# One more adder chunk on GpSimd, a new table of places in the attention loop, and weight halves awaited one by one

## The chip, the cores and the metric

The kernel runs on one core of a Trainium2 chip. The metric is device microseconds of one execution; before the change three runs gave a median of 1325.45 us (1325.14 to 1329.71). The engines are PE (TensorE), DVE (VectorE), ACT (ScalarE) and POOL (GpSimd); SP and ACT issue the DMAs.

## The reference

Two sequences of 1024 tokens with 1024 features go through one layer norm, then through an attention branch and a linear branch that are added to the input.

```
xn  = layernorm(x)
q, k, v = split(clip(xn @ Wqkv.T, -8, 8));  q, k = layernorm(q)*w+b, layernorm(k)*w+b
scores = q @ k.T / sqrt(32) + slope[h] * (pos_k - pos_q), causal     # 32 heads of 32
out = x + (softmax(scores) @ v) @ Wout.T + xn @ (alpha * sign(Wffn)).T + bias
```

## The kernel before, in words

**Blocks.** PE forms five products of 16 token tiles (128 tokens each) with 1024 x 1024 weights: F (the sign weights), Q, K, V, and after the attention the output product. `product` (L1079 on) goes over eight steps k; a step reads the two weight halves (columns 0 to 511 and 512 to 1023) of row block k, each kept as a high and a low fp16 part. ACT writes the high part (`split_hi`), DVE the low part (`split_lo`, L864, semaphore `w_lo`). Half number t of the next block is split while tile t of this block is worked on, after DVE has taken tile t out of PSUM (`clipped`, L940). Ahead of Q, of K and of V, PE waits until all 16 low halves are there. A product of tile t needs the PSUM banks of tile t-2 to be emptied.

**Attention.** 16 groups (n) of four heads follow. A group has 12 chunks c: chunks 0 to 3 are key tiles 0 to 3 of the first query half, chunks 4 to 11 are key tiles 0 to 7 of the second. A chunk is 512 query columns wide, or 384, 256 and 128 for the last tiles of a half (chunks 1, 2, 3 and 9, 10, 11). A place (c, j) is chunk c with head j. All engines go through fixed orders of work; semaphores alone tie them together. On PE, at each place:

- `scores` (L1206, with a mask product L1209 on the diagonal) writes one of three PSUM banks; it waits until the exponential (ACT, `exps`, L793) three places earlier has ended.
- 42 items of group n+1 are spread over the places of group n by `NATS`, the number of items in each chunk. 40 items are products (`maxima`, L1151) from which DVE takes row maxima (L988, L992); items 2 and 15 turn a row of them (L1158). They use three banks of their own: item i waits until DVE is done with item i-3. After item 41 DVE takes the minimum of two sets of 16 values (`both_halves`, L998), and item 2 of the next group's places waits for that minimum.
- `with_v` (L1229) multiplies the exponentials of a chunk with V into bank O, late, at the places that `PV_AFTER` gives (-2 and -1 are chunks 10 and 11 of the group before). The first of a group waits until ACT has copied bank O out for the last half (`os_copy` of half 1, L801). `DIRECT` chunks are also summed over keys by fp32 products with ones (L1235), into bank S.

**Sums on POOL.** For the chunks in `ADDED` POOL adds the exponentials into one tile (`add_in`, L641), and one product with ones (L1239, behind chunk 11's `with_v`) sums that tile. For the first half POOL adds chunks 1 and 2 to chunk 0 (`add_first`, L651), and `sums_first` (L1248) sums the result. The order on POOL in a group n > 0 is: `o_norm(n-1, 0)` (L620), add_first 1, add_first 2, `o_low(n-1, 0)` (L630), add 6, add 7 (chunk numbers), `o_norm(n-1, 1)`, add 9, `o_low(n-1, 1)`. `add_first` waits for the `with_v` of chunk 0. ACT's `os_copy(n, 0)` writes the buffer that `o_low(n-1, 0)` reads, and waits for it. Buffers of exponentials are reused: `HELD` names the chunk whose products and adds must be over before a chunk is written. Sums leave by `sums0_copy`, a DMA, `recips` on DVE, two more DMAs, and come back to `o_norm`.

Of the kernel before, what the change touches and what calls it, by code (L numbers as in the profile page):

```python
# [14 lines left out]
NT = TOK // P  # L15
KT = DM // P
QT = SEQ // P
# [12 lines left out]
def ready(n, ring=RING):  # L30

    return n + 1 + ring


def slot_free(n):

    return n + 1


def stored(j):  # L40


    return 16 * j + 16
# [23 lines left out]
def build_program(nc, x, wqkv_t, wout_t, wffn_t, ffn_bias, q_w, q_b, k_w, k_b,  # L67
# [9 lines left out]
    with ctx:  # L77
# [110 lines left out]
        def sem(name):  # L188
            return ctx.enter_context(nc.semaphore(name))
# [29 lines left out]
        w_lo = sem("w_lo")  # L219
# [49 lines left out]
        F, Q, K, V, WO = range(5)  # L269
# [20 lines left out]
        def span(c):  # L290
# [1 line left out]
            at = max(0, P * t - HALF * qb)  # L292
            return qb, t, at, HALF - at

        NATS = [3, 4, 3, 4, 3, 4, 4, 4, 5, 3, 2, 3]
        assert sum(NATS) == ITEMS


        PV_AFTER = {(0, 2): [-2], (2, 1): [-1], (3, 0): [0], (4, 2): [1], (5, 2): [2], (5, 3): [3],
                    (7, 1): [4], (8, 1): [5], (9, 0): [6], (9, 3): [7], (10, 2): [8], (11, 1): [9]}  # L300

        def due(c, j):

            return sum(NATS[:c]) + NATS[c] * (j + 1) // GH

        ADDED = (1, 2, 3, 5)
        DIRECT = [t not in (ADDED if qb else (0, 1, 2)) for qb, t in CHUNKS]
        ADDS = len(ADDED) - 1  # L310
        ADDS0 = 2
        FIRST_ADDS = {3: [1, 2]}

# [5 lines left out]
        def slot(c):  # L321
            i, col = SLOT[c]
            return p32[i][:, :, col:col + span(c)[3]]

        def adds_for(k):

            n, c = k // NC, k % NC
            return ADDS * n + max(1, ADDED.index(CHUNKS[c][1])) if CHUNKS[c] in [(1, t) for t in ADDED] else 0

# [20 lines left out]
        def need(eng, s, v):  # L350
            if v > 0:
                eng.wait_ge(s, v)
# [201 lines left out]
        def _(pool):  # L554
# [60 lines left out]
            def o_norm(n, qb):  # L615

                m = blk_no(n, qb)
                pool.wait_ge(r_ld[m % 2], 16 * (m // 2 + 1))
                o = os_sb[m % 2][:, 0, :]
                nc.gpsimd.tensor_tensor(o, o, rb[m % 2], ALU.mult).then_inc(on_done, 1)  # L620

            def o_low(n, qb):

                m = blk_no(n, qb)
                pool.wait_ge(oh_done, m + 1)
                if (n, qb) == (0, 0):
                    for s in range(2):
                        pool.wait_ge(v_st[s], stored(NT // 2))
                part = [ot[n][:, s, qb * HALF:(qb + 1) * HALF] for s in range(2)]
                nc.gpsimd.tensor_tensor(part[1], os_sb[m % 2][:, 0, :], part[0], ALU.subtract).then_inc(ol_done, 1)  # L630

            def add_in(n, c):

                qb, t, at, w = span(c)
                k = n * NC + c
                pool.wait_ge(exp_done, GH * (k + 1))
                if t == ADDED[1]:
                    need(pool, pv_done, n * NC)
                need(pool, add_done, adds_for(k) - 1)
                former = slot(c - 1) if t == ADDED[1] else acc[:, :, at:HALF]  # L640
                nc.gpsimd.tensor_tensor(acc[:, :, at:HALF], former, slot(c), ALU.add).then_inc(add_done, 1)  # L641

            def add_first(n, c):

                at = span(c)[2]
                k = n * NC + c
                pool.wait_ge(exp_done, GH * (k + 1))
                pool.wait_ge(pv_done, n * NC + 1)
                need(pool, add0_done, adds0_for(k) - 1)
                total = slot(0)[:, :, at:HALF]  # L650
                nc.gpsimd.tensor_tensor(total, total, slot(c), ALU.add).then_inc(add0_done, 1)  # L651

            for n in range(GROUPS):
                for c in range(NC):
                    if CHUNKS[c] in [(1, t) for t in ADDED[1:]]:
                        add_in(n, c)
                    for first in FIRST_ADDS.get(c, []):
                        add_first(n, first)
                    if n > 0:
                        if c == 0:  # L660
                            o_norm(n - 1, 0)
                        if c == 5:
                            o_low(n - 1, 0)
                        if c == 7:
                            o_norm(n - 1, 1)
                        if c == 11:
                            o_low(n - 1, 1)
            def resid(t):
                p = t % 2
# [20 lines left out]
        def _(act):  # L690
# [83 lines left out]
            for t in range(NT):  # L774
                p, j = t % 2, t // 2
# [46 lines left out]
            for n in range(GROUPS):  # L822
                for c in range(NC):
                    for j in range(GH):
                        exps(n, c, j)
                        if n > 0:
                            if (c, j) == (2, 1):
                                o_high(n - 1, 0)
                            if (c, j) == (2, 1):
                                os_copy(n - 1, 1)  # L830
                            if (c, j) == (11, 0):
                                o_high(n - 1, 1)
                            if j == 3 and 0 < c <= LOADS and n + 2 < GROUPS:
                                load_part(act, n + 2, c - 1)
                            if (c, j) == (LOADS + 1, 3) and n < GROUPS - 1:
                                if n == 1:
                                    for s in range(2):
                                        act.wait_ge(v_st[s], stored(NT // 2))
                                load_vg(act, n + 1)
                        if (c, j) == (6, 2):  # L840
                            os_copy(n, 0)
                        if (c, j) == (6, 2):
                            sums0_copy(n)
            os_copy(GROUPS - 1, 1)
            o_high(GROUPS - 1, 0)
# [4 lines left out]
        def _(dve):  # L850
# [168 lines left out]
            for t in range(NT):  # L1019
                p, j = t % 2, t // 2  # L1020
# [16 lines left out]
            for n in range(GROUPS):  # L1037
                for pos in range(ITEMS):
                    if n < GROUPS - 1:
                        nat_item(n + 1, pos)  # L1040
                    elif pos == 0:
                        row_out(n, use(GROUPS, 0), row_b, rowb_ld)
                    if pos == 18 and n > 0:
                        recips(n - 1, 1)
                    if pos == 33:
                        recips(n, 0)

            def c_out_step(t, p):
# [13 lines left out]
        def _(pe):  # L1062
# [41 lines left out]
            def block_product(blk, t, p, between=None, tile=None):  # L1104
                pe.wait_ge(mm_out, slot_free(t + NT * blk))
                product([ps[:, 2 * p + c, :] for c in range(2)],
                        lambda k, a: xnt[:, bass.ds(t if tile is None else tile, 1), k, a, :].rearrange("p o c -> p (o c)"),
                        wsl[blk % 2], TWO if blk == F else THREE, between).then_inc(mm_done, 1)
# [23 lines left out]
            pe.wait_ge(const_ld, 16 * 3)  # L1132
            pe.wait_ge(alpha_set, 1)

            for blk in (Q, K):
                pe.wait_ge(w_lo, ready(NT * blk - 1))

                def step(t, p, j, first=False):
                    block_product(blk, t, p, tile=p * QT + j)

                tile_loop(pe, step)

# [34 lines left out]
                    maxima(s, pos)  # L1177


            pe.wait_ge(w_lo, ready(NT * V - 1))  # L1180
            for t in range(NT):
                if t < V_FIRST:
                    block_product(V, t, t % 2)
                    continue
                if t == V_FIRST:
                    pe.wait_ge(fill_ld, 16 * 2 * STACKS)

                def between(k):
                    for pos in range(due_in_v(t, k - 1), due_in_v(t, k)):
                        nat_item(0, pos)  # L1190

                block_product(V, t, t % 2, between)
# [61 lines left out]
            for n in range(GROUPS):  # L1254
                pe.wait_ge(rowa_ld, ROW_PARTS * (n + 1))
                for c in range(NC):
                    if c == QB_END[0] + 1:
                        pe.wait_ge(rowb_ld, ROW_PARTS * (n + 1))
                    for j in range(GH):
                        scores(n, c, j)  # L1260
                        if n < GROUPS - 1:
                            for pos in range(due(c, j - 1), due(c, j)):
                                nat_item(n + 1, pos)
                        elif (c, j) == (0, 0):
                            row_b_turn(n, use(GROUPS, 0))
                        for late in PV_AFTER.get((c, j), []):
                            if n > 0 or late >= 0:
                                with_v(n * NC + late)
                        if (c, j) == (6, 2):
                            sums_first(n)  # L1270


# [77 lines left out]
```

## Time and profile before

| | before |
|---|---|
| median of 3 runs | 1325.45 us |
| profiled execution, its own time | 1327.45 us |
| its span | 1325.4 us |
| PE, DVE, POOL, ACT busy | 97%, 61%, 43%, 38% |
| mean granted TensorE clock | 0.995 |
| Q, K, V stages | about 147 to 671 us |
| attention | 672.7 to 1152.7 us |
| output product | to the end |

Busy is the share of the span in which an engine had an instruction running. PE's instructions are pipelined and their ends are modelled, so on PE the distance from one start to the next says more than a duration. "idle before" with a releaser names what ended an engine's wait.

### The profile page before, as it was taken

The numbers are of one execution on the slowest core, as the hardware profiler recorded it, in microseconds if no ns is written. First come the engines' busy times: TensorE is split into PE (matmuls) and PEld (weight loads), VectorE is DVE, ScalarE is ACT, GpSimd is POOL, SyncE is SP. The second block draws the span as 40 slices with busy tenths as digits, with TensorE's granted clock in tenths as the row PEclk, the third lists the DMA queues.
The fourth block names the chain that finished last, engine by engine and source line by source line (L and its number), as shares of the span: only waits on it lengthen the run. The fifth ranks groups of instructions, "written<-read, shape, count | busy, mean of one in ns | idle before, by whom it ended". The sixth has DMA issues, their size and how long they took to land.

```text
span 1325.4 us, 35664 instructions
## 1 busy us (share of the span) xinstructions
PE 1289.3 (97%) x14628; PEld 640.9 (48%) x14628; DVE 808.0 (61%) x1811; ACT 510.1 (38%) x1018; POOL 574.8 (43%) x360
## 2 busy tenths in 40 slices
PE   5999999998999989999999999999999999999998
PEld 3455444443444434444356655555555555444443
DVE  4656378876877772123688888888888888011111
ACT  6444011111111110000057777777777777600000
POOL 5562000000000000000037777777777777797674
PEclk9999999999999989999999999999999999999999
DMA  6545122222222225922114333444443331344443
GB/s 238 197 159 192 62 71 73 74 77 70 68 77 78 77 80 133 218 72 72 65 50 85 89 87 85 92 99 91 104 100 91 87 90 38 114 140 155 143 144 126
DMA packets 167718, 137.97 MB, mean 104 GB/s; under 512 B 116273, under 2 KB 132785, under 8 KB 167346
## 3 DMA queue, kind: packets, MB, share of 16 engines
q1 hardware_dynamic: 68020, 99.55, 25.2%
q10 hardware_dynamic: 99566, 36.50, 12.3%
q8 instruction: 102, 1.67, 0.6%
q14 instruction: 30, 0.25, 0.1%
HBM read 93.42 MB, written 42.21 MB: 102 GB/s over the span
## 4 chain that ended last, share of the span: by engine, by line
PE 94%; DVE 2%; DMA 1%; issue 1%; POOL 1%; ACT 1%; SPq 0%; DVEq 0%; ACTq 0%; POOLq 0%
PE ps L1085 59%; PE ps L1151 9%; PE ps L1206 9%; PE ps L1229 9%; PE ps L1235 3%; PE ps L1209 2%; PE ps L1074 1%; PE ps L1248 1%; PE ps L1239 1%; DMA arena<-arena 1%; DVE ps L988 1%; DMA arena<-in_x 0%; POOL arena L651 0%; SPq L470 0%; DVE arena L940 0%
## 5 line engine op out<-in xcount | busy, mean ns | idle before, releaser
L1085 PE MATMUL ps<-arena 128*128 128x512 f16 x3584 | 786.9, 381 | 9.3 <-DVE arena L864 9.0
L1085 PEld LDWEIGHTS ps<-arena 128*128 128x128 f16 (+1 forms) x3584 | 348.6, 98 | 434.7 <-issue 15.4
L793 ACT ACTIVATE arena<-ps 128x512 f32<-128x512 f32 (+3 forms) x768 | 333.1, 499 | 122.1 <-PE ps L1209 69.1
L988 DVE CUSTOM_DVE_ANT_0 ps<-ps,arena 128x128 f32<-128x128 f32 (+3 forms) x512 | 238.4, 517 | 37.0 <-PE ps L1151 36.8
L1206 PE MATMUL ps<-arena 128*32 128x512 f16 (+3 forms) x3072 | 256.8, 327 | 3.6 <-DVE arena L940 1.4
L1151 PE MATMUL ps<-arena 127*32 127x512 f16 (+3 forms) x3072 | 237.8, 328 | 0.6 <-DVE arena L988 0.4
L641 POOL TENSOR_TENSOR arena<-arena 128x2048 f32<-128x2048 f32 (+1 forms) x48 | 202.8, 4226 | 37.5 <-ACT arena L793 35.0
L651 POOL TENSOR_TENSOR arena<-arena 128x1536 f32<-128x1536 f32 (+1 forms) x32 | 93.8, 2930 | 262.5 <-PE ps L1229 190.0
L992 DVE TENSOR_REDUCE arena<-ps 128x1 f16<-128x512 f32 x256 | 166.7, 687 | 47.8 <-PE ps L1151 47.7
L564 POOL TENSOR_TENSOR small<-small 128x1 f32<-128x1 f32 x48 | 19.5, 407 | 386.6 <-DVE small L876 384.9
L1229 PE MATMUL ps<-arena 128*32 128x512 f32 (+3 forms) x1536 | 160.6, 486 | 0.5 <-issue 0.3
L940 DVE TENSOR_SCALAR arena<-ps 128x1024 f32<-128x1024 f32 x48 | 58.8, 1224 | 144.0 <-PE ps L1085 133.9
L1206 PEld LDWEIGHTS ps<-arena 128*32 128x32 f16 x3072 | 93.0, 96 | 76.5 <-issue 28.3
L751 ACT ACTIVATE arena<-arena 128x1024 f16<-128x1024 f32 x32 | 33.8, 1056 | 247.2 <-DVE arena L976 247.2
L1209 PE MATMUL ps<-arena 128*32 128x128 bf16 x2048 | 120.7, 218 | 0.0
L701 ACT ACTIVATE arena<-arena 128x512 f32 (+1 forms) x64 | 40.0, 627 | 205.3 <-DMA arena<-in_wout_t 151.5
L1052 DVE SCALAR_TENSOR_TENSOR arena<-ps,arena 128x1024 f32<-128x1024 f32 x16 | 19.6, 1224 | 152.6 <-PE ps L1085 130.0
L1151 PEld LDWEIGHTS ps<-arena 127*32 127x32 f16 x3072 | 83.9, 96 | 51.8 <-issue 14.6
L1209 PEld LDWEIGHTS ps<-arena 128*32 128x32 bf16 x2048 | 63.1, 97 | 47.1 <-issue 27.6
L988 DVE DVE_READ_ACCUMULATOR2_ANT arena<- 128x1 f16 x512 | 72.9, 142 | 0.0
L871 DVE BATCH_NORM_STATS2 small<-arena 128x6 f32<-128x512 f32 x96 | 61.6, 683 | 6.3 <-DMA arena<-in_x 5.2
L969 DVE SCALAR_TENSOR_TENSOR arena<-arena,small 128x1024 f32<-128x1024 f32 x32 | 41.1, 1284 | 33.3 <-POOL small L610 33.3
(55 smaller groups left out, 848.1 us busy)
## 6 DMA issues: line engine op xcount, KB each, us to landing
arena<-in_x SPq DMA_DIRECT2D x32, 512.0 KB, 5.3
arena<-in_wqkv_t SPq DMA_DIRECT2D x48, 256.0 KB, 6.1
base_scr<-arena SPq DMA_DIRECT2D x16, 512.0 KB, 2.9
v_scr<-arena SPq DMA_DIRECT2D x16, 512.0 KB, 3.0
arena<-r_scr SPq DMA_DIRECT2D x32, 256.0 KB
arena<-base_scr SPq DMA_DIRECT2D x16, 512.0 KB, 4.0
out_dram<-arena SPq DMA_DIRECT2D x16, 512.0 KB, 6.2
arena<-v_scr ACTq DMA_DIRECT2D x14, 512.0 KB, 4.2
```

Of the source, the lines that this page charges most:

```text
L641: nc.gpsimd.tensor_tensor(acc[:, :, at:HALF], former, slot(c), ALU.add).then_inc(add_done, 1)
L651: nc.gpsimd.tensor_tensor(total, total, slot(c), ALU.add).then_inc(add0_done, 1)
L793: nc.scalar.activation(slot(c)[:, j, :], ps[:, TRB[x % RB], 0:w], ACT.Exp, scale=SCALE).then_inc(exp_done, 1)
L871: ins = nc.vector.bn_stats(bst[p][:, 6 * c:6 * c + 6], xc[p][:, c * HALF:(c + 1) * HALF])
L940: nc.vector.tensor_scalar(dst[p], banks(2 * p, 2), lim, -lim, ALU.min, ALU.max)\
L988: ins = nc.vector.tensor_tensor_reduce(tile, tile, mnat[:, HALF - width:HALF], scale=-1.0, scalar=3e38, op0=ALU.add, op1=ALU.min, accum_ou ...
L992: ins = nc.vector.tensor_reduce(negm[s % 2][:, at:at + 1], tile, AX, ALU.max, negate=True)
L1085: ins = nc.tensor.matmul(dst[c], lhs(k, a), wparts[:, k, b, c * HALF:(c + 1) * HALF], start=(k == 0 and (a, b) == order[0]), stop=(k == KT ...
L1151: ins = nc.tensor.matmul(by_tile(dst), q[0:P - 1, r // DH, i, j], tiles_of(k[0:P - 1], j, key, width), start=True, stop=True)
L1206: ins = nc.tensor.matmul(by_tile(dst), k[:, r // DH, t, j], tiles_of(q, j, q0, w), start=True, stop=not diagonal)
L1209: ins = nc.tensor.matmul(dst[:, 0:P], idb[:, r:r + DH], mtr, start=False, stop=True)
L1229: ins = nc.tensor.matmul(dst(O_BANK, j, at), v[:, t, j, :], p[:, j, :], start=first, stop=last)
```

## The change

`ADDED` gets chunk (1, 6), which is chunk 10. So POOL also adds chunk 10 into the tile (256 columns for each of four heads), between add 9 and `o_low(n-1, 1)`; PE no longer forms chunk 10's four fp32 products with ones; PE's product L1239 waits for one add more, and ACT's chunk 2 of the next group, which reuses the buffer, waits for the add. `FIRST_ADDS`, and the places of `o_norm` and `o_low`, move in POOL's text, though except for the new add the order of POOL's instructions stays as it was. `NATS`, `PV_AFTER` and the places of ACT's and DVE's copies change. The wait for all 16 weight halves becomes a wait for each step's two halves in the first tile of Q, K and V.

```diff
-        NATS = [3, 4, 3, 4, 3, 4, 4, 4, 5, 3, 2, 3]
+        NATS = [2, 4, 2, 4, 4, 5, 5, 2, 3, 4, 5, 2]
-        PV_AFTER = {(0, 2): [-2], (2, 1): [-1], (3, 0): [0], (4, 2): [1], (5, 2): [2], (5, 3): [3],
-                    (7, 1): [4], (8, 1): [5], (9, 0): [6], (9, 3): [7], (10, 2): [8], (11, 1): [9]}
+        PV_AFTER = {(0, 2): [-2], (2, 2): [-1], (3, 0): [0], (3, 3): [1], (4, 3): [2], (5, 2): [3],
+                    (7, 2): [4], (8, 0): [5], (9, 0): [6], (9, 3): [7], (10, 2): [8], (11, 2): [9]}
-        ADDED = (1, 2, 3, 5)
+        ADDED = (1, 2, 3, 5, 6)
-        FIRST_ADDS = {3: [1, 2]}
+        FIRST_ADDS = {3: [1], 5: [2]}
@@ POOL: o_norm(n-1, 0), o_norm(n-1, 1), o_low(n-1, 1) in the loop over c
-   c == 0, c == 7, c == 11
+   c == 2, c == 8, c == 10
@@ ACT
-   o_high(n-1, 0) at (2, 1); os_copy(n-1, 1) at (2, 1); o_high(n-1, 1) at (11, 0)
+   o_high(n-1, 0) at (3, 2); os_copy(n-1, 1) at (2, 2); o_high(n-1, 1) at (10, 3)
-   os_copy(n, 0) at (6, 2); sums0_copy(n) at (6, 2)
+   os_copy(n, 0) at (6, 0); sums0_copy(n) at (6, 3)
@@ DVE
-                    if pos == 18 and n > 0: recips(n - 1, 1)      ... pos == 33: recips(n, 0)
+                    if pos == 19 and n > 0: recips(n - 1, 1)      ... pos == 34: recips(n, 0)
@@ PE
+            def weights(blk, k):
+                pe.wait_ge(w_lo, ready(NT * (blk - 1) + 2 * k + 1))
             for blk in (Q, K):
-                pe.wait_ge(w_lo, ready(NT * blk - 1))
+                weights(blk, 0)
                 def step(t, p, j, first=False):
-                    block_product(blk, t, p, tile=p * QT + j)
+                    block_product(blk, t, p, (lambda k: weights(blk, k + 1)) if first else None, p * QT + j)
-            pe.wait_ge(w_lo, ready(NT * V - 1))
+            weights(V, 0)                                          # and the same between in V's tile 0
-                        if (c, j) == (6, 2): sums_first(n)
+                        if (c, j) == (6, 1): sums_first(n)
```

## Rows read from the trace of the kernel before

**Rows 1.** Stretch of one attention group: length, busy time of each engine, clock, DMA.
```profile
1019.39:1049.45 30.06, 30.06 (x679) 16.82 (x674) 25.63 (x86) 23.57 (x56) 23.28 (x10) 1.00 0.42 93
```

**Rows 2.** Waits of PE: total us, times, longest.
```profile
PE ps L1085 <- DVE arena L864: 9.0, 2, 4.5
```

**Rows 3.** DVE in order of time, block ends: start, us, work [idle before].
```profile
302.12 1.22 DVE L940 TENSOR_SCALAR arena<-ps 128x1024 f32<-128x1024 f32 x1 [0.66 <-PE ps L1085]
...
312.48 1.22 DVE L940 TENSOR_SCALAR arena<-ps 128x1024 f32<-128x1024 f32 x1 [0.94 <-PE ps L1085]
...
328.96 1.23 DVE L940 TENSOR_SCALAR arena<-ps 128x1024 f32<-128x1024 f32 x1 [7.14 <-PE ps L1085]
...
484.36 1.23 DVE L940 TENSOR_SCALAR arena<-ps 128x1024 f32<-128x1024 f32 x1 [0.94 <-PE ps L1085]
...
502.03 1.22 DVE L940 TENSOR_SCALAR arena<-ps 128x1024 f32<-128x1024 f32 x1 [8.32 <-PE ps L1085]
...
524.23 1.22 DVE L940 TENSOR_SCALAR arena<-ps 128x1024 f32<-128x1024 f32 x1 [10.05 <-DMA v_scr<-arena]
```

**Rows 4.** Stretch behind the first wait: length, PE busy, granted clock, DMA, GB/s.
```profile
317.00:319.00 2.00, 2.00 (x5) 0.50 0.52 135
```

**Rows 5.** PE in order of time, a late group (product with V of chunk 4; then from place (0, 0)).
```profile
1021.28 1.04 PE L1229 MATMUL ps<-arena 128*32 128x512 f32 x8
...
1034.54 0.40 PE L1206 MATMUL ps<-arena 128*32 128x512 f16 x4
...
1036.13 0.61 PE L1235 MATMUL ps<-arena 128*32 128x256 f32 x8
1036.56 0.40 PE L1206 MATMUL ps<-arena 128*32 128x512 f16 x4
...
1036.84 0.22 PE L1158 MATMUL ps<-arena 128*16 128x128 f16 x1
...
1039.23 0.40 PE L1229 MATMUL ps<-arena 128*32 128x128 f32 x8
...
1041.54 1.04 PE L1229 MATMUL ps<-arena 128*32 128x512 f32 x8
```

**Rows 6.** POOL in order of time, the same group.
```profile
1021.93 9.34 POOL L641 TENSOR_TENSOR arena<-arena 128x2048 f32<-128x2048 f32 x2 [2.09 <-ACT arena L793]
...
1032.44 3.52 POOL L641 TENSOR_TENSOR arena<-arena 128x1536 f32<-128x1536 f32 x1
1035.90 1.17 POOL L630 TENSOR_TENSOR arena<-arena 128x512 f16<-128x512 f32 x1
...
1046.40 2.38 POOL L651 TENSOR_TENSOR arena<-arena 128x1024 f32<-128x1024 f32 x1 [0.17 <-POOL arena L651]
1048.74 1.16 POOL L630 TENSOR_TENSOR arena<-arena 128x512 f16<-128x512 f32 x1
```

**Rows 7.** DVE's minimum of the same group.
```profile
1035.76 0.23 DVE L998 TENSOR_TENSOR arena<-arena 128x16 f16<-128x16 f16 x1
```

**Rows 8.** An early group: DVE's minimum.
```profile
734.16 1.11 DVE L998 TENSOR_TENSOR arena<-arena 128x16 f16<-128x16 f16 x1
```

**Rows 9.** The early group: POOL.
```profile
734.05 1.19 POOL L630 TENSOR_TENSOR arena<-arena 128x512 f16<-128x512 f32 x1
```

**Rows 10.** All sixteen of DVE's minima: ns least/median/most, first and last start.
```profile
L998 DVE TENSOR_TENSOR arena<-arena x16: 167/222/1171, 671.0 to 1125.9; 128x16 f16<-128x16 f16 x16
```

**Rows 11.** The early group: PE, item 3.
```profile
735.97 0.40 PE L1151 MATMUL ps<-arena 127*32 127x512 f16 x4 [0.21 <-DVE arena L988]
```

**Rows 12.** The last group: ACT's copy of bank O behind chunk 11's product.
```profile
1131.67 0.60 ACT L801 ACTIVATE arena<-ps 128x512 f32<-128x512 f32 x1 [0.33 <-PE ps L1239]
```

**Rows 13.** The last group: PE, chunk 11's product with V, then chunk 0's.
```profile
1130.12 0.40 PE L1229 MATMUL ps<-arena 128*32 128x128 f32 x8
...
1132.37 1.07 PE L1229 MATMUL ps<-arena 128*32 128x512 f32 x8 [0.32 <-issue]
```

**Rows 14.** ACT in order of time, a late group: three exponentials.
```profile
1021.21 1.63 ACT L793 ACTIVATE arena<-ps 128x512 f32<-128x512 f32 x3
```

More of the change, by code:

```diff
@@ L659, in _ @@
                     if n > 0:
-                        if c == 0:
+                        if c == 2:
                             o_norm(n - 1, 0)
@@ L663, in _ @@
                             o_low(n - 1, 0)
-                        if c == 7:
+                        if c == 8:
                             o_norm(n - 1, 1)
-                        if c == 11:
+                        if c == 10:
                             o_low(n - 1, 1)
@@ L826, in _ @@
                         if n > 0:
-                            if (c, j) == (2, 1):
+                            if (c, j) == (3, 2):
                                 o_high(n - 1, 0)
-                            if (c, j) == (2, 1):
+                            if (c, j) == (2, 2):
                                 os_copy(n - 1, 1)
-                            if (c, j) == (11, 0):
+                            if (c, j) == (10, 3):
                                 o_high(n - 1, 1)
@@ L839, in _ @@
                                 load_vg(act, n + 1)
-                        if (c, j) == (6, 2):
+                        if (c, j) == (6, 0):
                             os_copy(n, 0)
-                        if (c, j) == (6, 2):
+                        if (c, j) == (6, 3):
                             sums0_copy(n)
@@ L1042, in _ @@
                         row_out(n, use(GROUPS, 0), row_b, rowb_ld)
-                    if pos == 18 and n > 0:
+                    if pos == 19 and n > 0:
                         recips(n - 1, 1)
-                    if pos == 33:
+                    if pos == 34:
                         recips(n, 0)
@@ L1177, in nat_item @@
                     maxima(s, pos)
-            pe.wait_ge(w_lo, ready(NT * V - 1))
+            weights(V, 0)
             for t in range(NT):
                 if t < V_FIRST:
-                    block_product(V, t, t % 2)
+                    block_product(V, t, t % 2, (lambda k: weights(V, k + 1)) if t == 0 else None)
                     continue
@@ L1268, in _ @@
                                 with_v(n * NC + late)
-                        if (c, j) == (6, 2):
+                        if (c, j) == (6, 1):
                             sums_first(n)
```

## The prediction

> **What bounds the kernel now.** I read the busy shares first, then one attention group as a stretch, then PE's waits, then each engine in order of time. PE is busy for the whole of a group and no other engine is: DVE 25.6, ACT 23.6, POOL 23.3 of 30.06 us [rows 1]. PE's only long waits outside the start are two of 4.5 us for DVE's weight halves [rows 2], at the ends of Q and K. So the time is PE's work plus what makes PE wait, and the question is what the shorter order makes late.
>
> **Weight halves, a gain.** While a block runs, DVE takes a tile out each 10.36 us (302.12 to 312.48). From Q's last tile to K's first it is 16.48 us, from K's last to V's first 17.67 us [rows 3]. The excess is 6.12 and 7.31 us, more than the 4.5 us of waiting, because PE works on at the lower of its two clocks behind the wait: 0.50 granted, and 5 products in 2 us [rows 4]. PE had stood idle before that. Only the last low half is late, since half t is split behind tile t. With step waits PE comes to it at 7/8 of a tile, 9.1 us behind the block's end, and it is ready 4.5 us behind it: no wait, no idle, no lower clock. Q's first tile gains nothing, as no wait stands there [rows 2]. What is late next? DVE takes V's tile 2 out only when a store has landed, at 524.23 [rows 3]; PE needs that bank for tile 4, which starts at 525.8 if V follows K at once (four tiles behind 484.36). Even if the store did not move this holds by some 0.3 us, and the stores' chain hangs on V's tile 0 and moves too. Price if that cover failed: 1 us. The step waits themselves I put at 0: tiles with a wait each follow at 10.36 us (bounds 0 and 24 x 0.1 us, an estimate from the 0.10 us between the copy's end at 1132.27 and PE's start behind it [rows 12, 13]). Sum: **-13.4 us** (bounds -13.4 and -11.0).
>
> **Chunk 10's sums leave PE.** Four products of 256 columns, 1036.13 to 1036.56: 0.43 us in each group [rows 5], 16 groups, -6.9 us, if nothing takes its place. POOL's new add has the shape of 1046.40: 2.38 us [rows 6], and 0.17 us behind the add before it. 23.3 + 2.4 of 30 us would fit by the sum; its place decides.
>
> **Where the new add lies.** I count in a steady group from E, the end of the exponential at (6, 3). Add 6 starts 0.08 us behind E; from its start to the end of add 9 it is 14.03 us (1021.93 to 1035.96) [rows 6]. So add 9 ends at E + 14.1, add 10 runs from E + 14.3 to E + 16.7. On PE, chunk 4's product with V moves from (7, 1) to (7, 2), behind a score that needs the exponential of (6, 3): it starts no earlier than E + 0.27: that score's 0.22 us and 0.05 from release to start, half of the 0.10 that rows 12 and 13 show behind a copy (at 0.10 the new add only comes earlier). From it to the next group's first score, call that S, it is 13.26 us (1021.28 to 1034.54) [rows 5], less the 0.22 us score that now lies ahead: 13.04. So S = E + 13.3, add 9 ends at S + 0.8, and **add 10 runs from S + 0.95 to S + 3.33**. Before, add 9 ended at S + 1.42 and a short `o_low` of 1.17 us followed.
>
> **Who meets it.** DVE's minimum (L998) is ready at S + 1.22 (1035.76) [rows 7]; item 41 keeps its place against S, so 1.2 again. Its row ends at 1035.99, 0.03 us behind add 9's end. In the early group it started 0.11 us after `o_low` and took 1.11 us, to 735.27, again 0.03 us behind POOL's end at 735.24 [rows 8, 9]. The 16 minima take 0.17 to 1.17 us for the same 16 columns [rows 10]. I take it that this instruction, which reads two SBUF operands, waits for the POOL instruction in flight. Then it ends at S + 3.33 instead of S + 1.45.
>
> The Trainium skill's page "SBUF — State Buffer", section "Who interferes with whom", says that a DVE instruction with two SBUF inputs contends with a GpSimd instruction that reads SBUF, and that whichever issues first keeps the shared pair for its whole length. By that rule the blocked sum below holds (about 1338 us); by the reading that the long minima are chance, the free sum does (about 1317 us). The rows' 0.03 us ends bear the rule out.
>
> **What PE does then.** PE comes to item 2's turn at S + 2.30 - 0.43 = S + 1.9 (1036.84 is 2.30 behind 1034.54) [rows 5] and must wait for the minimum: 3.4. Item 3 started 0.70 us after the minimum's end in the early group (735.97) [rows 8, 11], so S + 4.03. To chunk 11's product it is 1.7 us of scores and items by widths (0.42 ns a column, from the 0.43 us for 4 x 256) and 0.2 us for ACT's pace: S + 5.9. Chunk 0's product follows at least 2.25 us later, for bank O's copy must be over: 1130.12, copy at 1131.67, product at 1132.37 [rows 12, 13]. (Before it was 2.31 us, with more scores between [rows 5]; now scores alone would give 1.96.) So chunk 0's product is at S + 8.15. From its start to the end of `o_low(n-1, 0)` it is 8.36 us (1041.54 to 1049.90) [rows 5, 6]. `os_copy(n, 0)`, moved from behind the exponential of (6, 2) to behind (6, 0), must wait for that: +0.08. A copy takes 0.60 us and three exponentials 1.63 [rows 12, 14], of which I let 0.15 overlap: the next E is 10.5 us behind chunk 0's product, S + 18.65. The group: 18.65 + 13.3 = **31.95 us, 1.9 more than 30.05**.
>
> If the minimum were free, ACT's pace would put chunk 11's product at 4.69 (1039.23) - 0.43 + 0.17 = S + 4.43, chunk 0's at 6.68, E at 17.2 and the group at **30.5 us**: the two waits on ACT and `o_low` take back more than the 0.43 us. That is the nearer bound of the cost of this step; the far one is 29.62 us, if no wait comes at all.
>
> **Sum.** Groups 2 to 14: 13 x 1.9 = 24.7, less 1 us, since two early groups pay part of it already [rows 8]: 23.7. Group 1, where POOL has no `o_norm` of half 1 and add 10 lies 1.3 us earlier: +0.5. Group 0: 0. Group 15 waits for the minimum at its first place, 1.9 us later than now, then copy and `o_low` as above, and PE saves 0.43 in the tail: together +1.5 (0 to 3). Attention +25.7, weights -13.4: **+12.3 us**. The profiled execution reports 1327.45 us around a span of 1325.4; the median of runs, 1325.45, equals the span, so I put the change on the median: 1337.8 us, given as 1338. The output product is PE's own work; POOL's last add delays its residual sums by 2.4 us, and the first tile taken out still precedes PE's need of its banks: 0.
>
> **Rivals.**
> - *The minimum is free.* For it: add 10 precedes the minimum by only 0.25 us; if the minimum arrives in the 0.17 us between the adds it slips through. Against: PE cannot start chunk 4's product before E + 0.27, so add 9 can't end later than S + 0.8. 13 x 0.45 less the share of the early groups that goes, + 0.5 for groups 1 and 15: +5 - 13.4 = -8.4, 1317 us. Chance 0.17.
> - *Nothing waits at all.* -13.4 - 6.9 = 1305 us. For it: PE shows no idle in steady groups. Against: bank O's copy already leaves 0.06 us (2.31 against 2.25). Chance 0.08.
> - *Only the weight part's gain goes*, V's store or the lower clock keeping half of it, with the blocked groups: 1345 us. Against: rows 3 as above. Chance 0.05.
> - *Blocked*, the forecast: 0.70, with its own range 1331 to 1343 (a group 31.4 to 32.3 us). It is the case on the slower side: from the point where add 10 starts ahead of the minimum, each group pays the rest of 2.38 us.
>
> **How the numbers follow.** The range reaches from the free case to the top of the blocked one: 1316 to 1343 us. Half a per cent, 6.6 us, is about what a measurement of this kernel tells from no change. Faster than 1318.8: the second rival and some two thirds of the first, 0.20. Within: the rest of the first and the blocked case's lower edge, 0.15. Slower than 1332.1: 0.65.
>
> **What would show it.** Right: DVE's tiles 10.4 us apart over both block ends, no lower clock there; L998 2 us long in groups 2 to 14, ending with a POOL add of 1024 columns; PE's L1158 about 3.4 us behind the group's first score; groups of about 32 us. Wrong: L998 at 0.2 us (then 30.5 or less for a group), `os_copy(n, 0)` starting without a wait, or an idle PE in V.

## The result, and the profile after

The changed kernel takes **1338.4 us** (median of four runs, 1337.9 to 1338.6), the kernel before beside it on the same chip 1327.1. The ratio is **1.008 (95%: 1.006 to 1.011)**: slower by 0.8%. The forecast was 1338 us, from an expected +12.3 us on 1325.45; between the two medians here it is +11.3 us, between the profiled spans 1336.9 - 1325.4 = +11.5 us. All readings below are of the profiled execution.

The busy shares, one engine after the other, for the whole span of the changed kernel: PE is at 97%, and nobody else has come near it.
```profile
PE 1291.8 (97%) x14500; PEld 617.6 (46%) x14500; DVE 828.6 (62%) x1811; ACT 509.5 (38%) x1018; POOL 610.4 (46%) x376
```

One group of attention in the columns of [rows 1], from one group's first score nearly to the next one's. PE is no longer busy throughout: 1.4 us of idle are new. POOL is 2.15 us busier, by the new add, and DVE 1.6 us, though it has no new work.
```profile
1005.15:1037.00 31.85, 30.42 (x670) 15.82 (x666) 27.23 (x86) 23.62 (x54) 25.43 (x11) 1.00 0.38 88
```

PE's waits (total us, times, longest), to be read against [rows 2]: the wait for L864 is gone, and one for the minimum, L998, has come.
```profile
PE ps L1162 <- DVE arena L998: 14.4, 12, 2.8
PE ps L1155 <- DVE arena L988: 2.6, 12, 0.2
```

**Where time was gained.** DVE's tiles taken out, where [rows 3] had the gaps: the last of K stands at 477.86 and the first of V at 488.32, 10.46 us apart where it was 17.67. Q's and K's tiles pass through at 10.36. The tile that waits for V's store (the last row) has moved forward by 11.7 us, from 524.23 to 512.54, nearly as far as the chain, and PE waits nowhere in V.
```profile
301.74 1.23 DVE L940 TENSOR_SCALAR arena<-ps 128x1024 f32<-128x1024 f32 x1 [0.65 <-PE ps L1085]
312.10 1.23 DVE L940 TENSOR_SCALAR arena<-ps 128x1024 f32<-128x1024 f32 x1 [0.94 <-PE ps L1085]
...
477.86 1.23 DVE L940 TENSOR_SCALAR arena<-ps 128x1024 f32<-128x1024 f32 x1 [0.94 <-PE ps L1085]
488.32 1.23 DVE L940 TENSOR_SCALAR arena<-ps 128x1024 f32<-128x1024 f32 x1 [1.12 <-PE ps L1085]
...
512.54 1.23 DVE L940 TENSOR_SCALAR arena<-ps 128x1024 f32<-128x1024 f32 x1 [12.07 <-DMA v_scr<-arena]
```

The stretch of [rows 4], read in the same way: 11 products in 2 us where there were 5, at a granted clock of 1.00 (2.4 GHz) where it was 0.50.
```profile
317.00:319.00 2.00, 2.00 (x11) 1.00 0.60 145
```

DVE takes V's last tile out 13.7 us earlier, at 657.70 against 671.41, and PE's first score of attention is as far ahead: 658.97 against 672.69.

**Where it was lost.** PE in the same order as [rows 5], in the group that begins at S = 1005.15. The turn of item 2 (L1162) waits 1.05 us for the minimum; the products with V (L1233) of chunks 11, 0 and 4 stand at 1011.00, 1013.24 and 1024.07.
```profile
1005.15 0.40 PE L1210 MATMUL ps<-arena 128*32 128x512 f16 x4
...
1008.46 0.22 PE L1162 MATMUL ps<-arena 128*16 128x128 f16 x1 [1.05 <-DVE arena L998]
...
1009.12 0.40 PE L1155 MATMUL ps<-arena 127*32 127x512 f16 x4 [0.21 <-DVE arena L988]
...
1011.00 0.40 PE L1233 MATMUL ps<-arena 128*32 128x128 f32 x8
...
1013.24 1.07 PE L1233 MATMUL ps<-arena 128*32 128x512 f32 x8 [0.15 <-issue]
...
1024.07 1.03 PE L1233 MATMUL ps<-arena 128*32 128x512 f32 x8
...
1037.10 0.40 PE L1210 MATMUL ps<-arena 128*32 128x512 f16 x4
```

POOL in the same stretch, against [rows 6]. One row holds adds 9 and 10; it ends at 1008.38.
```profile
1002.40 5.98 POOL L641 TENSOR_TENSOR arena<-arena 128x1536 f32<-128x1536 f32 x2
1008.34 1.16 POOL L630 TENSOR_TENSOR arena<-arena 128x512 f16<-128x512 f32 x1
```

DVE's minimum of this group, against [rows 7]: ready at S + 1.13, 2.13 us long for the same 16 columns, over at 1008.41, 0.03 us behind POOL.
```profile
1006.28 2.13 DVE L998 TENSOR_TENSOR arena<-arena 128x16 f16<-128x16 f16 x1
```

All sixteen minima, against [rows 10]: the median went from 222 to 2129 ns.
```profile
L998 DVE TENSOR_TENSOR arena<-arena x16: 168/2129/2144, 657.3 to 1134.1; 128x16 f16<-128x16 f16 x16
```

From group to group, by the start of POOL's row that holds `add_first` 2, the fifteen lengths sum to 453.8 us before and 477.8 after. Before they are 31.1, 30.7, 30.7, then 30.0 to 30.1, at the end 30.7. After they are 31.9 to 32.1, with two of 30.53 and 30.54 (groups 2 and 10), and 33.3 at the end. In the two short ones the minimum slipped through, as here (DVE, then POOL's row of adds 9 and 10, then add 10 by itself): it started between the two adds, 0.02 us ahead of add 10.
```profile
721.51 0.17 DVE L998 TENSOR_TENSOR arena<-arena 128x16 f16<-128x16 f16 x1
```
```profile
717.91 6.02 POOL L641 TENSOR_TENSOR arena<-arena 128x1536 f32<-128x1536 f32 x2
```
```profile
721.53 2.40 POOL L641 TENSOR_TENSOR arena<-arena 128x1024 f32<-128x1024 f32 x1
```
The minimum was no earlier there (S + 1.13, as elsewhere); add 10 was later, at S + 1.15 instead of S + 0.88. The delay begins between adds 6 and 7 of the groups just before (1 and 9): they stand 0.44 us apart there and 0.14 us in all others (one row). Group 9, then group 10:
```profile
966.39 4.58 POOL L641 TENSOR_TENSOR arena<-arena 128x2048 f32<-128x2048 f32 x1 [0.43 <-ACT arena L793]
```
```profile
991.92 9.30 POOL L641 TENSOR_TENSOR arena<-arena 128x2048 f32<-128x2048 f32 x2 [2.23 <-ACT arena L793]
```
The exponential that the row names was over by 964.92, so it is not what add 7 waited for. The same pause of 0.3 us stands in groups 1 and 9, and in no other, of all ten kernels in which POOL adds chunk 10 as one instruction, and in no group of the other four (before, e1, e5, e6). What makes it is not known.

The last group, beside [rows 13]: the turn waits 2.83 us there, and a product with ones (L1252) 0.47 for POOL's last add.
```profile
1136.20 0.22 PE L1162 MATMUL ps<-arena 128*16 128x128 f16 x1 [2.83 <-DVE arena L998]
...
1149.63 1.07 PE L1252 MATMUL ps<-arena 128*32 128x384 f32 x16 [0.47 <-POOL arena L651]
```

### The profile page after: what moved, and what is told of

Same layout as the page of the kernel before. It is cut to its first block, busy times and chain, and to the rows that moved or that the text cites. A ratio compares the mean times of both kernels' runs of the same rounds, so it can differ in the third digit from the quotient of the medians.

```text
span 1336.9 us, 35440 instructions
## 1 busy us (share of the span) xinstructions
PE 1291.8 (97%) x14500; PEld 617.6 (46%) x14500; DVE 828.6 (62%) x1811; ACT 509.5 (38%) x1018; POOL 610.4 (46%) x376
## 4 chain that ended last, share of the span: by engine, by line
PE 91%; DVE 5%; issue 2%; ACT 1%; DMA 1%; POOL 0%; SPq 0%; DVEq 0%; ACTq 0%; POOLq 0%
PE ps L1085 58%; PE ps L1155 9%; PE ps L1233 8%; PE ps L1210 8%; PE ps L1239 3%; DVE ps L988 2%; PE ps L1213 1%; PE ps L1074 1%; DVE arena L998 1%; PE ps L1252 1%; PE ps L1243 1%; ACT arena L793 1%; DVE arena L992 1%; DVE arena L988 0%; DMA arena<-arena 0%
## 5 line engine op out<-in xcount | busy, mean ns | idle before, releaser
L641 POOL TENSOR_TENSOR arena<-arena 128x2048 f32<-128x2048 f32 (+1 forms) x64 | 239.9, 3749 | 43.3 <-ACT arena L793 38.8
L1155 PE MATMUL ps<-arena 127*32 127x512 f16 (+3 forms) x3072 | 228.9, 328 | 3.6 <-DVE arena L988 2.6
L992 DVE TENSOR_REDUCE arena<-ps 128x1 f16<-128x512 f32 x256 | 162.8, 688 | 36.3 <-PE ps L1155 35.0
L1233 PE MATMUL ps<-arena 128*32 128x512 f32 (+3 forms) x1536 | 159.4, 487 | 2.9 <-issue 2.2
L1210 PEld LDWEIGHTS ps<-arena 128*32 128x32 f16 x3072 | 88.0, 96 | 78.5 <-ACT arena L793 48.0
L1155 PEld LDWEIGHTS ps<-arena 127*32 127x32 f16 x3072 | 78.4, 95 | 78.5 <-DVE arena L988 28.1
L1213 PEld LDWEIGHTS ps<-arena 128*32 128x32 bf16 x2048 | 59.5, 97 | 46.9 <-issue 29.9
```

The costliest lines, as they stand in the source:

```text
L992: ins = nc.vector.tensor_reduce(negm[s % 2][:, at:at + 1], tile, AX, ALU.max, negate=True)
L1155: ins = nc.tensor.matmul(by_tile(dst), q[0:P - 1, r // DH, i, j], tiles_of(k[0:P - 1], j, key, width), start=True, stop=True)
L1210: ins = nc.tensor.matmul(by_tile(dst), k[:, r // DH, t, j], tiles_of(q, j, q0, w), start=True, stop=not diagonal)
L1213: ins = nc.tensor.matmul(dst[:, 0:P], idb[:, r:r + DH], mtr, start=False, stop=True)
L1233: ins = nc.tensor.matmul(dst(O_BANK, j, at), v[:, t, j, :], p[:, j, :], start=first, stop=last)
```

## The experiments

Each ran beside the kernel before. The ratio is to that kernel, with its 95% interval. "Step waits" are the change's weight waits alone; all kernels below but e2 have them. The table puts one late group of each kernel (about 1000 to 1060 us) into four stretches, from starts on PE: the group's first score, the product with V of chunk 11 (of the group before), of chunk 0, of chunk 4, the next first score.

| kernel | places | add 10 | minimum | to chunk 11 | to chunk 0 | to chunk 4 | to the score | group |
|---|---|---|---|---|---|---|---|---|
| before | old | no | two operands | 4.69 | 2.31 | 9.79 | 13.26 | 30.05 |
| after | new | yes | two | 5.85 | 2.24 | 10.83 | 13.03 | 31.95 |
| e3 | new | yes | one | 4.44 | 2.24 | 10.83 | 13.03 | 30.54 |
| e4 | old | yes | two | 4.26 | 3.30 | 9.82 | 13.27 | 30.65 |
| e8 | old, `o_high` later | yes | one | 4.28 | 2.29 | 9.80 | 13.26 | 29.63 |
| e9 | new, late ones undone | yes | one | 4.45 | 2.24 | 10.57 | 13.25 | 30.51 |
| e10 | new, early ones undone | yes | one | 4.27 | 2.25 | 10.82 | 13.02 | 30.36 |
| e11 | new, items old | yes | one | 4.72 | 2.24 | 11.01 | 12.96 | 30.93 |
| e12 | as e9, items old | yes | one | 4.72 | 2.25 | 9.98 | 13.41 | 30.36 |

**e1: the weight waits alone.** The kernel before with
```
- pe.wait_ge(w_lo, ready(NT * blk - 1))
+ weights(blk, 0)      # and weights(blk, k + 1) before step k + 1 of the first tile
```

> The kernel before with the step waits for weight halves alone. All theories: DVE takes tiles out 10.36 us apart over both block ends (before 16.48 and 17.67), no lower clock there; 13.4 us less than before, ratio 0.990. If the table or the add interacts with it, the difference of this run and the next from the whole change would not add up.

1314.65 us, ratio 0.990 (0.987 to 0.993). From Q's tile at 303.75 to V's first at 490.33 it is 186.58 us, 13.3 less than before, as in the changed kernel. Groups are 30.05 us, as before, but for one more of 30.6 (group 10), in which the minimum took 1.16 us. The clock behind Q's end, in the columns of [rows 4]:
```profile
317.00:319.00 2.00, 2.00 (x11) 1.00 0.25 86
```
The weight part is a gain of its own, and the only part of the change that is one as it stands.

**e2: the table alone.** The changed kernel with the old wait for the last half: the edit of e1 reversed.

> The changed kernel with the old wait for all weight halves: the add on POOL and the new places alone. If the parts are independent: 25 us more than before, ratio 1.019, groups of 31.8 us, L998 at 2.13 us. If the gain at the block ends were not what the changed kernel shows, this run would stay near it (ratio 1.008).

1353.49 us, ratio 1.020 (1.018 to 1.022). Waits of PE:
```profile
PE ps L1158 <- DVE arena L998: 14.5, 12, 2.8
PE ps L1085 <- DVE arena L864: 9.0, 2, 4.5
```
The two parts do not touch: 0.990 x 1.020 = 1.010 beside the whole change's 1.008 (1.006 to 1.011). DVE's tiles over the two block ends are 17.71 us (314.86 to 332.57) and 16.61 us (487.97 to 504.58) apart here, where the kernel before had 16.48 and 17.67 [rows 3]: the same two waits, but the dearer one now comes first.

**e3: the changed kernel, the minimum with one operand.** The two rows of 16 that the minimum compares lie side by side, so one reduction over a strided view gives the same result, into columns of its own:
```
- nc.vector.tensor_tensor(negm[n % 2][:, 16:32], negm[n % 2][:, 16:32], negm[n % 2][:, 32:48], ALU.min)
+ nc.vector.tensor_reduce(negb[n % 2], negm[n % 2][:, 16:48].rearrange("p (a b) -> p b a", a=2), AX, ALU.min)
```

> The changed kernel, but DVE forms the minimum as a reduction over one strided operand into its own 16 columns, in place of an operation with two SBUF operands. Port theory (the two-operand instruction waits for the POOL instruction in flight): the minimum takes 0.2 to 0.3 us, PE no longer waits for it, groups fall from 31.8 to 30.5 us, and the whole is 8 us less than before (ratio 0.994). Rival (the moved places cost the time, and the minimum's length is a symptom): no change, ratio 1.008. Rival (DVE or SBUF is slow for any instruction beside POOL's add): the reduction takes 2 us as well, ratio 1.008.

1321.01 us, ratio 0.996 (0.994 to 0.997), groups 30.53 us. All sixteen, then the one of a late group, and POOL beside it:
```profile
L999 DVE TENSOR_REDUCE arena<-arena x16: 185/187/189, 657.6 to 1118.5; 128x16 f16<-128x32 f16 x16
```
```profile
1026.61 0.19 DVE L999 TENSOR_REDUCE arena<-arena 128x16 f16<-128x32 f16 x1
```
```profile
1022.73 6.02 POOL L642 TENSOR_TENSOR arena<-arena 128x1536 f32<-128x1536 f32 x2
```
The reduction starts and ends in the middle of POOL's second add (1026.4 to 1028.75) and takes 0.19 us. So the 2.13 us were neither the work of a minimum nor a semaphore's delay, and DVE is not slow beside POOL's add in general. The edit changes three things at once, though: the number of SBUF operands, the operation, and the place of the result (no longer over an operand). The runs alone do not say which of them counts. This one instruction is worth 17.4 us (1338.4 to 1321.0), more than the change costs.

The Trainium skill's page "SBUF — State Buffer", section "Who interferes with whom", says this of both forms: `tensor_tensor` with both inputs in SBUF contends with GpSimd's reads, `tensor_reduce` on trn2 never does. The runs agree: 2129 ns in the median against 187 ns, under the same add. That the two operands are what counts rests on this page.

**e4: the new add in the old places.** The kernel before with the step waits and `ADDED = (1, 2, 3, 5, 6)`, nothing moved.

> The kernel before with step waits and with chunk 10 added on POOL, all places as in before, the two-operand minimum kept. Port theory: add 9 still ends 1.4 us behind a group's first score, the minimum is ready at 1.2 and goes between the two adds, so it takes 0.2 to 0.3 us; but the add delays o_norm(n-1, 0) by 2.5 us to 6.4 us, o_high stands before the copy of bank O at (2, 1), and chunk 0's product comes at 7.7 in place of 6.6: groups of 30.7 us, 4 us less than before in all (ratio 0.997). Rival (POOL's larger load costs it wherever the places are): L998 of 2 us, groups near 31.8, ratio 1.008. Rival (nothing waits with the old places): groups of 29.6, ratio 0.985.

1319.4 us, ratio 0.994 (0.992 to 0.996). The minimum is ready just before add 9 ends and goes first (DVE; then POOL, where the first add of the row ends at about 1029.92):
```profile
1029.72 0.25 DVE L998 TENSOR_TENSOR arena<-arena 128x16 f16<-128x16 f16 x1
```
```profile
1026.44 6.01 POOL L641 TENSOR_TENSOR arena<-arena 128x1536 f32<-128x1536 f32 x2
1032.42 1.17 POOL L630 TENSOR_TENSOR arena<-arena 128x512 f16<-128x512 f32 x1
1033.54 1.28 POOL L620 TENSOR_TENSOR arena<-arena 128x512 f32<-128x512 f32 x1
```
What is late instead is `o_high(n-1, 0)` at (2, 1): ACT stands 1.51 us there for POOL, and chunk 0's product behind it waits (ACT, then PE).
```profile
1034.86 0.63 ACT L817 ACTIVATE arena<-arena 128x512 f16<-128x512 f32 x1 [1.51 <-POOL arena L620]
```
```profile
1036.07 1.07 PE L1233 MATMUL ps<-arena 128*32 128x512 f32 x8 [0.82 <-issue]
```
So the add does not pay in the old table as it stands, for a reason that has nothing to do with the minimum: in the table above the second stretch is 3.30 us instead of 2.31.

**e5: the changed kernel, add 10 in two.** In `add_in`, the last of `ADDED` as two instructions of two heads each:
```
+ for js in (slice(0, 2), slice(2, 4)):
+     ins = nc.gpsimd.tensor_tensor(acc[:, js, at:HALF], acc[:, js, at:HALF], slot(c)[:, js], ALU.add)
+ ins.then_inc(add_done, 1)
...
```

> The changed kernel with add 10 given as two POOL instructions, one for heads 0 and 1 and one for heads 2 and 3; the two-operand minimum kept. Port theory, held for one instruction: the minimum waits for the first of the two only, so it takes about 1.0 us in place of 2.13, PE's turn of item 2 comes at 2.3 us behind the group's first score in place of 3.3, groups of 30.8 us, ratio to before 0.998. Rival (the minimum waits until POOL's queue is empty or until add 10's semaphore is given, for some ordering reason): 2.1 us or more, ratio 1.008 or above.

1326.21 us, ratio 1.000 (0.999 to 1.001); groups 30.87 us. DVE, then POOL:
```profile
1032.55 1.06 DVE L1003 TENSOR_TENSOR arena<-arena 128x16 f16<-128x16 f16 x1
```
```profile
1032.30 2.52 POOL L642 TENSOR_TENSOR arena<-arena 128x512 f32<-128x512 f32 x2
```
The minimum waits for the half that is in flight and no longer for the whole: the length of POOL's instruction sets its time.

**e6: the new places without the add.** The changed kernel with `ADDED = (1, 2, 3, 5)`.

> The changed kernel without the add: all new places and the step waits, but PE forms chunk 10's sums as before. Add 9 still ends 0.8 us behind the first score, o_low (1.17 us) follows, and the minimum, ready at 1.1 to 1.2, waits for it. Port theory: the minimum takes 0.8 us, groups of 30.9 us, ratio 1.000. If the new places cost nothing of themselves: 30.05 us, ratio 0.990 as with the weight waits alone. If they cost all: 31.8 us and more, ratio 1.012.

1328.39 us, ratio 1.001 (1.000 to 1.002); groups 30.83 us. DVE, then POOL, which is over at 1030.17:
```profile
1029.40 0.78 DVE L998 TENSOR_TENSOR arena<-arena 128x16 f16<-128x16 f16 x1
```
```profile
1029.00 1.17 POOL L630 TENSOR_TENSOR arena<-arena 128x512 f16<-128x512 f32 x1
```
The table alone, with no added work on POOL, already takes back all that the step waits give (30.83 against 30.05 us in a group). Under a short POOL instruction the minimum takes 0.78 us, but it is not what costs the group: chunk 11's product stands at S + 4.73, where it was S + 4.69, and the 0.8 us come between chunk 0's product and chunk 4's (10.84 us for 9.79, of which the next stretch gives 0.23 back).

**e7: the add with one place moved.** The kernel before, the step waits, the add, and of the new places only `o_high(n-1, 0)`: `(2, 1)` becomes `(3, 2)`.

> The kernel before with step waits, the add of chunk 10, all old places but one: o_high(n-1, 0) on ACT moves from (2, 1) to (3, 2), out of the way of the copy of bank O. The two-operand minimum is kept and goes between the adds (0.25 us). If the late o_high was all that the add cost with the old places: chunk 0's product no longer waits, groups of 29.8 us, 17 us less than before, ratio 0.987. If another wait stood behind it (the add's result for chunk 2 of the next group, needed at 4 us behind the first score): 30.2 or more, ratio 0.990 or above.

1311.96 us, ratio 0.990 (0.986 to 0.993). Most groups are 29.6 to 29.8 us, as expected; two that nobody expected are 32.1 (by POOL's `add_first` 2; 31.7 between first scores). There the minimum came 0.05 us behind add 10's start (DVE, then POOL's row, then add 10 by itself):
```profile
899.42 2.33 DVE L998 TENSOR_TENSOR arena<-arena 128x16 f16<-128x16 f16 x1
```
```profile
895.74 5.99 POOL L641 TENSOR_TENSOR arena<-arena 128x1536 f32<-128x1536 f32 x2
```
```profile
899.37 2.36 POOL L641 TENSOR_TENSOR arena<-arena 128x1024 f32<-128x1024 f32 x1
```
Whether a group pays hangs on one or two tenths of a microsecond. Each of the two groups follows one in which PE stood 0.3 us ahead of chunk 4's scores for a transfer of the row that item 2 turns, for the second as here:
```profile
968.66 0.62 PE L1210 MATMUL ps<-arena 128*32 128x512 f16 x8 [0.34 <-DMA arena<-arena]
```
PE's next first score came later by that and POOL's adds did not: from add 6 to the next first score it is 12.93 us in both, 12.6 us in the other late groups. So add 10 came first. That the transfer is the cause is read from the order of the rows; no run takes it away.

**e8: the same with the minimum of one operand.** e7 and the edit of e3.

> The same with the minimum as a one-operand reduction. Port theory: only the first few groups, where a POOL instruction lies over the minimum, gain: 0 to 1.5 us less than the run before this one, ratio 0.986.

1308.51 us, ratio **0.985 (0.983 to 0.988)**: faster than the kernel before by 1.5% and than the changed one by 2.2% (1308.5 / 1338.4). One group, in the columns of [rows 1]:
```profile
1000.00:1029.62 29.62, 29.62 (x674) 16.31 (x668) 25.39 (x86) 23.28 (x55) 25.60 (x11) 1.00 0.42 94
```
PE is busy for all of it, with 0.43 us less than before: here the add gives what was expected of it, and no more can be had from it. Against e7 the medians differ by 3.4 us, above the 0 to 1.5 expected. In the profiled executions e8 is 5.9 us shorter from group 1's first score to group 15's: the minimum costs e7 2.1 us in each of its two blocked groups, 1.0 us in group 1 and 0.3 us in group 10. Before attention e8's execution happens to be 3.0 us longer.

**e9 to e12: which place costs the rest?** With the minimum free, the new places still take 0.9 us more than e8 (30.53 against 29.63). e9 is e3 with `os_copy(n, 0)` and `sums0_copy(n)` back at (6, 2) and chunk 4's product at (7, 1):
```
- (7, 2): [4]
+ (7, 1): [4]
```

> The changed kernel with the one-operand minimum, and the places of the group's later half put back: ACT's two copies behind the exponential of (6, 2), chunk 4's product with V at (7, 1). The first chain theory: with the minimum free, 0.6 of the 0.9 us by which its groups (30.51 us) exceed PE's bare order (29.62) come from os_copy(n, 0) waiting for o_low(n-1, 0) and from chunk 4's product standing behind a score that needs (6, 3)'s exponential. Then groups of 29.9 us, ratio 0.989. Rival (the added scores pace, ACT's rate early in the group, costs most): groups stay above 30.3, ratio 0.994.

1320.78 us, ratio 0.995 (0.993 to 0.997), groups 30.51: no gain, and a miss. From chunk 0's product to chunk 4's it is 10.57 us instead of 10.83, where the kernel before has 9.79, and the next stretch is longer by 0.22. PE's weight loads for items wait for DVE's maxima (waits in 850 to 1050 us, total, times, longest; in e3 it is 5.0 us in 21 waits):
```profile
PEld ps L1156 <- DVE arena L993: 6.5, 28, 0.3
```
e12, below, has the old item counts beside the same places, and there this wait is 0.8 us in 5 times.

e10 is e3 with chunk 11's product and the copies at (2, 1):
```
- (2, 2): [-1]      and  (c, j) == (2, 2): os_copy(n - 1, 1)
+ (2, 1): [-1]      and  (c, j) == (2, 1): os_copy(n - 1, 1)
```

> The changed kernel with the one-operand minimum, and chunk 11's product with V and the copies of banks O and S behind it back at (2, 1); the later half as changed. By the same theory chunk 11's product comes 0.15 us sooner, still with 2.25 us to chunk 0's product behind it, and the chain from there is unchanged: groups of 30.35 us, ratio 0.994. If the early half held most of the 0.9 us: 29.9, ratio 0.989.

1317.51 us, ratio 0.992 (0.990 to 0.994), groups 30.36: the first stretch gives back its 0.17 us, and nothing else moves.

e11 is e3 with the old number of items in each chunk:
```
- NATS = [2, 4, 2, 4, 4, 5, 5, 2, 3, 4, 5, 2]
+ NATS = [3, 4, 3, 4, 3, 4, 4, 4, 5, 3, 2, 3]
```

> The changed kernel with the one-operand minimum and the items spread as before (the old NATS), all other new places kept. The run before last showed groups of 30.5 us with the later half's chain taken out, and PE waiting for DVE in chunks 5 and 6, where the new list has 10 items for 8 before. Two floors theory: the chain over o_low and the copies alone holds 10.8 us between chunk 0's and chunk 4's product with V, and so does DVE's pace in chunks 5 and 6; taking out one leaves the other: groups of 30.5 us, ratio 0.995. If the items were the only cost: 30.0 us or less, ratio 0.990.

1325.42 us, ratio 0.999 (0.997 to 1.000), groups 30.93: worse than e3, where 30.5 was expected.

e12 is e9 with the old `NATS`.

> Both taken out: one-operand minimum, old item list, and the later half's copies and chunk 4's product at their old places; chunk 11's product and the copies behind it stay at (2, 2). Two floors theory: 30.0 us a group (29.6 us of PE's order, 0.2 for ACT's pace, 0.3 for bank O's copy), 0.5 us less than either alone, ratio 0.989. If a third wait of the same height stands behind them: 30.5 us, ratio 0.995.

1316.61 us, ratio 0.992 (0.989 to 0.995), groups 30.36 instead of the 30.0 expected. The stretch to chunk 4 is nearly back (9.98 us), but the first is 0.28 us longer than e3's, one more item lying ahead of chunk 11's product at (2, 2), and then ACT stands for that product:
```profile
1027.13 0.60 ACT L802 ACTIVATE arena<-ps 128x512 f32<-128x512 f32 x1 [1.17 <-PE ps L1244]
```
In the stretch to chunk 4, the late places undone alone give 0.26 us, the item counts alone take 0.18, both together give 0.85; in the whole group it is 0.02, -0.4 and 0.17. The parts don't add up, and how the 0.9 us divide over single places stays open.

## Why the prediction was right

**Weight halves: right.** Forecast -13.4 us. From the tile taken out at 302.12 to V's first at 502.03 it was 199.91 us [rows 3]; it is 186.58 after (301.74 to 488.32), -13.3. V's end is 13.7 us ahead because the first block also began 0.4 us earlier in this run. e1's ratio, 0.990, is -13.4 us (-9.7 to -17.1). The excess over the waits that was put down to the lower clock went with them. V's store moved forward by 11.7 us, so the rival that half the gain is lost failed. The step waits cost next to nothing: with them K's first tile follows at 10.36 us, V's at 10.46. What each place costs beyond its wait can't be told from one trace, though: e2 has the two excesses the other way round. Their sum is nearly the same (13.4 us before, 13.6 in e2).

**The minimum behind add 10: right in mechanism and size.** Counted from S, forecast and measured: minimum ready 1.2 and 1.13; over 3.33 and 3.26; turn of item 2 3.4 and 3.31; item 3 4.03 and 3.97; chunk 11's product 5.9 and 5.85; chunk 0's 8.15 and 8.09; chunk 4's 18.65 + 0.27 = 18.92 and 18.92; the group 31.95 and 31.95. e3 takes the cause away and leaves the add: 30.53 us, the free case's forecast of 30.5. e5 halves the POOL instruction and the minimum halves. The rival "minimum free" is a real state of the kernel, in two groups of fifteen, of 30.53 and 30.54 us. The argument against it was wrong: it said that add 9 can't end later than S + 0.8, and in these two groups it ended at S + 1.0, for POOL had paused between adds 6 and 7 (the second add of the row at 717.91 starts at 721.53). The margin was put at 0.25 us (add 10 at S + 0.95, the minimum at S + 1.2), was 0.25 us (0.88 and 1.13), and the pause is 0.3.

**Four products of 256 columns: right.** With the add and chunk 11's product at its old place the first stretch is 4.26 to 4.28 us where it was 4.69 (e4, e8, e10), 0.41 to 0.43 less. "Nothing waits at all", forecast at 29.62 us a group and 1305 us, is what e8 reaches with 29.63 and 1308.5; it needed another minimum and other places.

**The sum: right in total, with small terms off.** Attention was forecast at +25.7 us. From its first score to the first output product it is 479.96 us before (672.69 to 1152.65) and 505.59 after (658.97 to 1164.56): +25.6. The terms, from first score to first score: groups 2 to 14 +20.7 (forecast 23.7), since thirteen blocked groups were counted and two were free (-2.8 us); group 0 +0.6 (0); group 1 +0.6 (0.5); group 15 +3.7 (1.5). So the agreement to a tenth is luck. The term for the last group was undersized: up to chunk 11's product it lost 1.8 us, as forecast, but then 1.3 us more up to chunk 4's product and 0.6 us behind it, where the forecast had -0.4 in all.

**What the prediction did not see** is how the loss splits. It took the waits on ACT and on `o_low`, its step from the free case's 30.5 to 29.62, as following from the new places one by one. e9 to e12 show that they don't: the stretch between chunk 0's and chunk 4's products also hangs on where the items stand: in e9 PE's weight loads wait for DVE's maxima in chunks 5 and 6, with the old item counts (e12) hardly, and the stretch goes from 10.57 to 9.98 us.

## What to carry to other kernels

Before work is put on POOL, list the DVE instructions with two SBUF operands that will fall under it, however short they are: each can last as long as POOL's instruction, and what waits for it pays. Here, rewriting the small one to read one operand (a reduction over a strided view of both rows) was worth 17 us under a POOL instruction whose place had not been touched. And test the parts of an order written by hand singly: here the moved places cost at least what the moved work could have given, and the part with the gain, a wait for the last of eight pieces cut into eight, had nothing to do with them.

## What the runs showed of the hardware

- DVE's minimum of 16 columns takes 0.17 us free and 0.78, 1.06 or 2.13 us under a POOL instruction of 1.17, 1.28 or 2.4 us (e6, e5, the changed kernel). Where POOL's row ends with the instruction that it waits for, it ends 0.01 to 0.03 us behind it; the wait stands in the trace as the DVE instruction's length and not as idle time before it.
- Between two POOL adds with nothing to wait for there is a gap of some 0.14 to 0.17 us, and what counts is which of the two engines starts first: a minimum 0.02 us ahead of add 10 took 0.17 us (721.51, changed kernel), one 0.05 us behind it 2.33 us (899.42, e7). One that was ready before add 9's end ran in the gap and took up to 0.25 us.
- POOL paused 0.3 us longer than elsewhere between adds 6 and 7 of groups 1 and 9, in ten kernels out of fourteen, with the same text of the loop in every group. The cause is open.
- Behind 4.5 us of idle PE ran at 1.2 GHz, a granted clock of 0.50 [rows 4]. The excess beyond the wait itself was 1.6 us at the first place (16.48 - 10.36 - 4.5) and 2.8 at the second (17.67 - 10.36 - 4.5) [rows 2, 3]; in e2, with the same waits of 4.5 us, it was 2.9 and 1.8. It went with the idle time.
